# Sorted expert tiles: a ring of eight weight and row buffers instead of six, and a queue that issues a pair's weights ahead of later rows

## The reference, cut to what matters

```python
def moe_ffn(x2d, w_router, w_gate_up, w_down):      # x2d: all 2048 tokens,
    logits = x2d @ w_router                         # 192 channels
    probs = jax.nn.softmax(logits, axis=-1)
    vals, idx = jax.lax.top_k(probs, 2)
    vals = vals / jnp.sum(vals, axis=-1, keepdims=True)
    combine = jnp.sum(jax.nn.one_hot(idx, 16) * vals[..., None], axis=1)
    out = jnp.zeros_like(x2d)
    for e in range(16):
        gu = x2d @ w_gate_up[e]                     # 192 -> 2 x 384
        gate, up = jnp.split(gu, 2, axis=-1)
        h = jax.nn.silu(gate) * up
        out = out + combine[:, e:e + 1] * (h @ w_down[e])   # 384 -> 192
    return out
```

## Time and profile before

| | |
|---|---|
| runs | 1249.12, 1249.82, 1258.29 us; median 1249.82 us |
| profiled execution | 1249.4 us |
| its span | 1247.3 us |
| PE busy | 1023.5 us (82%) |
| DVE, ACT, POOL busy | 739.1, 492.8, 322.3 us |
| sorted experts, gate and up matmuls with 128 rows of weights (L2098) | 72.4 us busy, 19.8 us idle before them |

### The profile page before, as it was taken

How to read it: one execution, slowest core, us unless ns; L and a number is a source line. 1 busy time by engine, 2 the same in 40 slices (tenths; PEclk the granted TensorE clock), 3 DMA queues, 4 the chain that set the end, 5 groups by cost and what they waited for, 6 DMA issues and landing times.

```text
span 1247.3 us, 26074 instructions
## 1 busy us (share of the span) xinstructions
PE 1023.5 (82%) x9535; PEld 799.4 (64%) x9574; DVE 739.1 (59%) x2287; ACT 492.8 (40%) x1225; POOL 322.3 (26%) x516
## 2 busy tenths in 40 slices
PE   4899999999998799675888878787876668988891
PEld 3677776776776455464666657575664447888891
DVE  6586586686674244254577777777766675332334
ACT  1452452553543222032465455555554553212110
POOL 0000000000000640167444463636101213222331
PEclk8999999999998899987999999999998989999996
DMA  9152241341341999200000000000000027788875
GB/s 351 28 144 72 72 143 54 89 143 34 109 143 56 295 405 415 60 1 1 1 2 1 19 1 19 1 19 2 18 2 18 18 89 272 269 275 288 289 260 168
DMA packets 69045, 144.80 MB, mean 116 GB/s; under 512 B 4896, under 2 KB 55360, under 8 KB 66656
## 3 DMA queue, kind: packets, MB, share of 16 engines
q1 hardware_dynamic: 64352, 132.88, 31.6%
q0 software_dynamic: 4608, 10.79, 2.6%
HBM read 97.35 MB, written 46.30 MB: 115 GB/s over the span
## 4 chain that ended last, share of the span: by engine, by line
PE 39%; DVE 27%; issue 19%; ACT 6%; POOL 5%; DMA 4%; POOLq 0%; DVEq 0%; ACTq 0%; SPq 0%
DVE neg_max L714 5%; PE bank L1830 4%; PE bank L569 3%; PE bank L614 3%; PE bank L636 3%; PE bank L1967 3%; PE bank L1858 2%; PE bank L808 2%; PE bank L678 2%; DVE R L687 2%; DMA R<-in_ffn_gu 2%; PE bank L815 2%; POOL sorted_x L1069 2%; PE bank L1917 2%; ACT R L743 1%
## 5 line engine op out<-in xcount | busy, mean ns | idle before, releaser
L743 ACT ACTIVATE R<-bank,neg_max 128x128 f32<-128x128 f32 (+2 forms) x576 | 188.7, 403 | 143.8 <-DVE neg_max L714 143.7
L1057 POOL TENSOR_SCALAR R<-cf,ids_rel 128x128 bf16<-128x128 f32 x256 | 170.1, 681 | 0.3
L614 PE MATMUL bank<-cf,R 128*128 128x128 f32 x864 | 136.6, 282 | 28.9 <-ACT R L752 15.2
L714 DVE TENSOR_REDUCE neg_max<-bank 128x2 f32<-128x352 f32 (+2 forms) x216 | 129.9, 608 | 31.1 <-PE bank L597 25.5
L614 PEld LDWEIGHTS bank<-cf,R 128*128 128x128 f32 x864 | 96.6, 144 | 47.4 <-ACT R L743 33.1
L1009 POOL TENSOR_TENSOR rstd<-mean_var,cf 128x2 f32<-128x2 f32 x24 | 4.7, 194 | 461.1 <-DVE mean_var L871 461.1
L766 ACT ACTIVATE R<-bank 128x1024 bf16<-128x1024 bf16 x72 | 70.5, 1020 | 78.9 <-PE bank L569 78.5
L1830 PE MATMUL bank<-R 64*116 64x256 f32 (+1 forms) x512 | 97.8, 399 | 0.0
L569 PE MATMUL bank<-cb,R 128*128 128x128 bf16 x1008 | 70.6, 234 | 28.9 <-DVE R L554 28.8
L569 PEld LDWEIGHTS bank<-cb,R 128*128 128x128 bf16 x1008 | 65.3, 106 | 36.6 <-DVE R L554 27.3
L2098 PE MATMUL bank<-xsT,R 128*128 128x128 f32 x576 | 72.4, 279 | 19.8 <-DMA R<-in_ffn_w 19.3
(11 more groups left out here) (258 smaller groups left out, 1940.9 us busy)
## 6 DMA issues: line engine op xcount, KB each, us to landing
R<-in_ffn_w SPq DMA_DIRECT2D x48, 864.0 KB, 6.7
sorted_x<-cmp SPq DMA_DIRECT2D x8, 4128.0 KB, 15.9
R<-in_ffn_gu SPq DMA_DIRECT2D x16, 1392.0 KB, 21.0
R<-in_ffn_dn SPq DMA_DIRECT2D x16, 768.0 KB, 17.8
xs_words<-sorted_x SPq DMA_DIRECT2D x48, 129.0 KB, 4.0
R<-token_y SPq DMA_DIRECT2D x8, 384.0 KB, 6.0
rows<-R SPq DMA_DIRECT2D x8, 224.0 KB, 2.3
out_x<-x_all SPq DMA_DIRECT2D x16, 96.0 KB, 2.4
```

Source lines behind the costliest of these rows:

```text
L614: ins = nc.tensor.transpose(PT[u % 2][:, at + g * P:at + (g + 1) * P], probs[:, u % 3, g * kw + c0:g * kw + c0 + P], ident)
L714: nc.vector.tensor_reduce(neg_max[:, u % 4, 0:g], score_bank(a, u)[:, 0:g * kw].rearrange("p (g k) -> p g k", g=g), AX, ALU.max, negate=Tr ...
L743: ins = nc.scalar.activation(probs[:, u % 3, g * kw:(g + 1) * kw], score_bank(a, u)[:, g * kw:(g + 1) * kw], ACT.Exp, bias=neg_max[:, u % ...
L1057: ins = nc.gpsimd.tensor_scalar(comb_s[:, t, j, :], cst("iota_tok"), ids_rel[:, j:j + 1], None, ALU.is_equal)
```

## The change

`WRING` becomes 8: both rings get two more slots. The weights ring grows inside the large buffer `R` by 2 x 1728 words a partition, `xs_words` by 2 x 258 words. `TURN` becomes 8, so that a turn is a whole number of times round the ring: six turns instead of four.

SP's program is written anew. At the beginning it issues the weights of tiles 0 to 7 and the rows of tiles 0 to 7 without a wait for a buffer, with the weights of tile 3 ahead of rows 2; then rows 8 to 11, weights 8 to 11, and the wait for the table as before. In the loop it issues, for each pair, first the weights of t + 8 and t + 9 (each waits for `f_y` of the tile eight before) and then the rows of t + 12 and t + 13.

To stay within the memory, four work tiles of the tables have 36 entries instead of 48, and the semaphores of the weights ring are those of layer 0's ring, counted on from there (`weights_landed`). Apart from these semaphores and from the number of turns, the other engines' instructions stay as they are, in their order.

```diff
-WRING = 6
-TURN = 12
+WRING = 8
+TURN = 8
...
-        cmp2 = sb("cmp2", [P, NSORT, E1])
+        cmp2 = sb("cmp2", [P, NSORT - EARLY, E1])
...
+        def weights_landed(j, k):
+
+            pairs = len(range(j // 2, NPAIR, RING))
+            return 16 * pairs + 16 * k + 16
...
                 sp.dma_start(w1_ring[j], d["ffn1_w"][bass.ds(expert, 1)].rearrange("a p w -> (a p) w"))\
-                    .then_inc(s(f"w1_loaded{j}"), 16)
+                    .then_inc(s(f"ring{j}"), 16)
...
             for t in (0, 1):
                 load_rows(t, t)
-            for t in (1, 2):
+            for t in (1, 2, 3):
                 load_weights(t, t)
-            for t in (2, 3):
+            for t in range(2, WRING):
                 load_rows(t, t)
-            load_weights(3, 3)
-            for t in (4, 5):
-                load_rows(t, t)
-            for t in (4, 5):
+            for t in range(4, WRING):
                 load_weights(t, t)
...
-            for t in range(WRING):
+
+            def weights_ahead(t, j):
+                load_weights(t + WRING, j, lambda: sp.wait_ge(s("f_y"), t + 1))
+            for t in range(EARLY - WRING):
                 rows_ahead(t, t)
-            for t in range(WRING):
-                load_weights(t + WRING, t, lambda: sp.wait_ge(s("f_y"), t + 1))
+            for t in range(EARLY - WRING):
+                weights_ahead(t, t)
...
-            for t in range(EARLY - WRING, WRING + 4):
-                rows_ahead(t, t % WRING)
+            for t in range(EARLY - WRING, WRING):
+                rows_ahead(t, t)
...
                 for j in range(j0, TURN, 2):
+                    t = n * TURN + j
                     for r in range(2):
-                        if more or j + r + 4 + WRING < TURN:
-                            rows_ahead(n * TURN + j + r + 4, (j + r + 4) % WRING)
-                    for r in range(2):
-                        t = n * TURN + j + r
-                        if more or j + r + WRING < TURN:
-                            load_weights(t + WRING, (j + r) % WRING, lambda: sp.wait_ge(s("f_y"), t + 1))
-            f_body(0, True, WRING)
-            turns(sp, NSORT // TURN, f_body, first=1)
+                        if more:
+                            weights_ahead(t + r, j + r)
+                    for r in (4, 5):
+                        if more and (more != "last" or j + r < TURN):
+                            rows_ahead(t + r, (j + r) % WRING)
```

More of the change, by code:

```diff
@@ L357, in build @@
         cmp = sb("cmp", [P, E1, 16])
-        cmp2 = sb("cmp2", [P, NSORT, E1])
-        cmp3 = sb("cmp3", [P, NSORT, E1])
+        cmp2 = sb("cmp2", [P, NSORT - EARLY, E1])
+        cmp3 = sb("cmp3", [P, NSORT - EARLY, E1])
         slot_g = sb("slot_g", [P, 2, E1])
@@ L363, in build @@
         slots_i = sb("slots_i", [P, 2, 2], I32)
-        tile_e = sb("tile_e", [P, NSORT])
+        tile_e = sb("tile_e", [P, NSORT - EARLY])
         tile_ei = sb("tile_ei", [P, NSORT], I32)
-        tile_b = sb("tile_b", [P, NSORT])
+        tile_b = sb("tile_b", [P, NSORT - EARLY])
         tile_bi = sb("tile_bi", [P, NSORT], I32)
@@ L442, in build @@
             s(f"b_rows{j}")
-        for j in range(RING):
-            s(f"ring_gu{j}")
-            s(f"ring_dn{j}")
+        for j in range(2 * RING):
+            s(f"ring{j}")
         for r in range(2):
@@ L448, in build @@
                 s(f"{n}{r}")
-        for j in range(WRING):
-            s(f"w1_loaded{j}")
         for j in range(WRING):
@@ L907, in load_gate_up @@
             def load_gate_up(j):
-                sp.dma_start(ring_gu[j % RING], d["ffn0_gu"][j]).then_inc(s(f"ring_gu{j % RING}"), 16)
+                sp.dma_start(ring_gu[j % RING], d["ffn0_gu"][j]).then_inc(s(f"ring{2 * (j % RING)}"), 16)
             def load_down(j):
-                sp.dma_start(ring_dn[j % RING], d["ffn0_dn"][j]).then_inc(s(f"ring_dn{j % RING}"), 16)
+                sp.dma_start(ring_dn[j % RING], d["ffn0_dn"][j]).then_inc(s(f"ring{2 * (j % RING) + 1}"), 16)
             for j in range(2):
@@ L971, in rows_ahead @@
                 load_rows(t + WRING, j, lambda: (sp.wait_ge(s("f_xT"), t + 1), sp.wait_ge(s("f_place"), t + 1)))
-            for t in range(WRING):
+            def weights_ahead(t, j):
+                load_weights(t + WRING, j, lambda: sp.wait_ge(s("f_y"), t + 1))
+            for t in range(EARLY - WRING):
                 rows_ahead(t, t)
-            for t in range(WRING):
-                load_weights(t + WRING, t, lambda: sp.wait_ge(s("f_y"), t + 1))
+            for t in range(EARLY - WRING):
+                weights_ahead(t, t)
             sp.wait_ge(s("e_tiles"), 2)
             sp.wait_ge(s("scattered"), 64 * B)
-            for t in range(EARLY - WRING, WRING + 4):
-                rows_ahead(t, t % WRING)
+            for t in range(EARLY - WRING, WRING):
+                rows_ahead(t, t)
             def f_body(n, more, j0=0):
                 for j in range(j0, TURN, 2):
+                    t = n * TURN + j
                     for r in range(2):
-                        if more or j + r + 4 + WRING < TURN:
-                            rows_ahead(n * TURN + j + r + 4, (j + r + 4) % WRING)
-                    for r in range(2):
-                        t = n * TURN + j + r
-                        if more or j + r + WRING < TURN:
-                            load_weights(t + WRING, (j + r) % WRING, lambda: sp.wait_ge(s("f_y"), t + 1))
-            f_body(0, True, WRING)
-            turns(sp, NSORT // TURN, f_body, first=1)
+                        if more:
[3 more added lines that the diff above has]
+                            rows_ahead(t + r, (j + r) % WRING)
+            f_body(0, True, EARLY - WRING)
+            with sp.Fori(1, NSORT // TURN - 2) as n:
+                f_body(n, True)
+            f_body(NSORT // TURN - 2, "last")
             for r in range(2):
@@ L1910, in b_gate_up @@
                     w = ring_gu[j % RING]
-                    pe.wait_ge(s(f"ring_gu{j % RING}"), 16 * (j // RING) + 16)
+                    pe.wait_ge(s(f"ring{2 * (j % RING)}"), 16 * (j // RING) + 16)
                     if r == 0:
@@ L1943, in b_body @@
                     w = ring_dn[j % RING]
-                    pe.wait_ge(s(f"ring_dn{j % RING}"), 16 * (j // RING) + 16)
+                    pe.wait_ge(s(f"ring{2 * (j % RING) + 1}"), 16 * (j // RING) + 16)
                     for c in range(DC0):
@@ L2093, in f_gate_up @@
                 for r in range(2):
-                    pe.wait_ge(s(f"w1_loaded{(j + r) % WRING}"), 16 * (n * (TURN // WRING) + (j + r) // WRING) + 16)
+                    pe.wait_ge(s(f"ring{(j + r) % WRING}"), weights_landed((j + r) % WRING, n * (TURN // WRING) + (j + r) // WRING))
                     w = w1_ring[(j + r) % WRING]
```

## The result

| kernel | runs | median us | lowest to highest | ratio to before [95%] |
|---|---|---|---|---|
| before, in the same comparison | 20 | 1250.72 | 1247.41 to 1259.95 | |
| the change | 20 | 1245.31 | 1229.51 to 1255.29 | 0.9923 [0.9901, 0.9944] |
| the change, second comparison | 6 | 1246.29 | 1241.81 to 1251.52 | 0.9923 [0.9895, 0.9951] |

The ratios leave out executions more than 1.5% above the fastest of the same kernel, which are five of the change's first 20 and no other here; the medians and the lowest and highest times leave out none. By the ratio the change makes the kernel 0.8% faster. By the medians it is 0.4% in the first comparison (5.4 us) and 0.7% in the second, from which nothing is left out (8.4 us, against 1254.69 for the kernel before).

A forecast was written before the change was run, and what follows sets the result against it. It took weight loads asked for too late as what holds PE in the sorted experts' stage. Gains of 23.7 us less 1.9 (table) and 1.9 (scatter) gave 19.9 off 1249.4, so 1230 us, range 1224 to 1243.

The forecast's parts named there:

- Loop, lead: Steady loop: weights asked for earlier, right at `f_y`, arrive before PE wants them; gain 19.0 us, lower bound nothing.
- the slow matmuls: Loop before the change: 24 matmuls of L2105 once took 2.93 us instead of 1.61; 1.3 us not counted as gain.
- Beginning: Start of the stage: weights of tiles 6 and 7 are issued earlier and land before PE wants them; gain 4.7 us.
- Loop, traffic: Steady loop: a pair's 2.23 MB takes 5.9 us at 376 GB/s, below the 6.76 us body.
- the first rival: Steady loop: the transfers set the pace at 7.4 us a body, losing 12.3 us of the gain; 1242 us, chance 0.14.
- Second and fourth rivals: Table's delay not caught up until tile 20, 1236 us, chance 0.10; lead does nothing as loads land later, 1247, 0.07.
- Rows after weights: Loop: rows issued some 2.3 us later in the body still land before PE transposes them; cost nothing.
- rows 2 and 3: Beginning: these rows, now behind the weights of tile 3, land by 1034.9, before their transposes; cost nothing, at most 3.3 us.
- The table: SP's lead is cut once by waiting for the table; tile 13's weights come late, costing 1.9 us, between nothing and 3.8.
- Scatter of y: Scatters and copy of y hide behind PE's body, except while SP catches up behind the table; 1.9 us, between nothing and 4.
- In that gap the scatter lands early: Loop: a late copy delays `f_y` and the next weights, leaving a gap for the scatter; its shortest landing is 2.3 us.
- the third rival: Loop: scatters become the bound, DVE's copy of y waits, every turn takes 8.69 us; 1261 us, chance 0.07.

The follow-up runs named there:

- two y: The change with room for a second pair of y, used by turns, against the kernel before: ratio 0.9801, median 1225.41 us.
- the weights held: The change, but the weights of t + 8 wait until POOL has issued the second scatter of pair t - 2: ratio to the kernel before 0.9841, 1232.21 us.
- three kernels with two y and eight buffers: The change with a second pair's room for y: alone, with the table's rest entered earlier, or with rows issued first; ratios to before 0.9801, 0.9786, 0.9795.
- six, weights first: The kernel before with its six buffers, but SP issues a pair's weights ahead of the rows: ratio 0.9921, 1242.42 us.
- rows first: The change with eight buffers, but SP issues a pair's rows ahead of its weights, as before: ratio to the kernel before 0.9895, 1238.06 us.
- the two held kernels: The change with weights waiting for the second scatter's issue, without and with the table's rest entered earlier: ratios to the kernel before 0.9841 and 0.9828.

## Why the prediction was wrong

- **Loop, lead (19.0 us): right.** With two y the loop takes 148.72 - 129.1 = 19.6 us less, of which 1.3 are the slow matmuls. In the change the waits for weights go as well, but the loop takes 148.58 us, only 0.1 less.
- **Beginning (4.7 us): right.** 18.27 us became 13.52. Weights 6 and 7 are among the four that SP issues from 1037.31 on.
- **Loop, traffic, and the first rival: right to reject it.** 0.90 of the DMA engines are busy at 321 GB/s, and bodies are at 6.76 us.
- **Second and fourth rivals: right to reject them.** The change waits for weights twice, at tiles 12 and 13, and no more; 3.7 us are left of 19.3.
- **Rows after weights, rows 2 and 3: right, nothing.** No matmul of L2092 waits for rows.
- **The table (1.9 us): too small.** It cost 4.2. I had SP issue its rows again 1072.7 - 1063.4 = 9.3 us ahead of PE's tile 12. In the trace they go out at 1067.96 and tile 12 would come at 1068.64 + 6.76 = 1075.4, only 7.4 us later. With two y the wait is 0.4 us: the surplus belongs to the next point.
- **"Scatter of y" (1.9 us): this step failed.** The bodies behind the table lost 15.9 us and not 1.9. The prediction let the copy come "1.4 us after the next down projection: more room than now", since the weights would land early. It took from the earlier trace rows that a scatter lands with the weights beside it, and then let PE's body set the turn. But the copy, the scatter's issue and its landing follow one another: the second scatter is issued 2.37 us after the copy, and where weights went out 0.3 us ahead of it it was seen landed 4.6 to 7.0 us after that, so the next copy can't come sooner than 7.0 to 9.4 us after the last. All of that is more than the 6.76 of a body.
- **"In that gap the scatter lands early", the argument against the third rival: half true.** In the turns with late copies it holds for a pair's first scatter (2.4 to 3.0 us). The second, issued 1.38 us later, falls behind the weights, and the copy waits for both. So a late copy is not made up for. The experiment with the weights held puts that gap back in every other turn, and that is enough.
- **The third rival was the right mechanism, with too high a price.** It had turns of 8.69 us and 1261. Bodies from tile 14 on take 7.75, since turns with a wait (9.38) stand beside others without, and 4.7 us of the beginning stay won.

The sizes add up: of the difference between the stage's predicted 181.2 - 19.9 = 161.3 us and its 176.5, y has 15.9 - 1.9 = 14.0, the table 4.2 - 1.9 = 2.3, and the 1.3 us of slow matmuls that I had left in is to be taken off: 15.0 of 15.2.

The prediction weighed two rules of the Trainium skill, page "DMA: Bandwidth & Descriptors", section "Queues, rings and completion order". By the one, that a DMA engine takes turns between its queues packet by packet, the second scatter had little to fear from the 1.77 MB in SP's queue; here its 6.8 us from issue to landing, beside 2.35 for the first, speak against it as the whole story. By the other, that an increment lands after every earlier write of its engine, a landing is tied to the weights under way; 6.8 us behind the weights and 2.35 ahead of them agree with it. I gave that one 7 in 100. Whether write order or the queues' turns make the 6.8 us no run here tells apart.

Open: why the change's executions spread over 1229.51 to 1255.29 us, while each of the three kernels with two y and eight buffers stays within 5.6 to 7.3 us. Two profiles of the change agree in kind, but both are of executions above the median, at 1247.21 and 1251.52 us, and none is of one near 1230: what the fast executions do is not known, and the 15.9 us are those of a slower one. The other kernel with weights first, one pair of y and nothing held (six, weights first) spreads widely too, 17.1 us in 8 executions, while rows first and the two held kernels stay within 4.1 to 5.8 us in 5 or 6. That fits a spread that comes with the waits for y, but it is an argument, not shown.

## What to carry to other kernels

When loads are issued earlier, list every other transfer that the same event sets off and see which is issued first: a small store issued 0.3 us behind the first of 1.77 MB of loads took 4.4 us longer to land than its twin issued 1.04 us ahead of them. If its source has one buffer, its turn (copy, issue, landing) sets the pace once it is longer than the engine's body. Either give it a second buffer (here 384 words a partition for 1.2% more) or let the loads wait until it is issued (0.8%).

## What the runs showed of the hardware

Two things I had not expected. Two 128x192 scatters issued 1.38 us apart land after very different times: in the nine turns of the change whose weights went out 2.02 to 2.05 us after the copy, the first, about 1.04 us ahead of the weights, was seen landed after 2.4 to 3.0 us, the second, about 0.34 us behind, after 4.6 to 7.0. It is not that whichever is issued first wins. In this turn of the change the second scatter was 0.41 us ahead of the weights and still was seen landed only after 5.5 us:

```profile
1163.41 0.99 POOL L1103 DMA_INDIRECT token_y<-y_f,place_i  x1 [0.16 <-POOL scratch L1102]
1163.82 1.49 SPq L949 DMA_DIRECT2D R<-in_ffn_w  x2
...
1168.93 0.16 DVE L1769 TENSOR_TENSOR place_i<-places,cf 128x1 int32<-128x1 f32 x1 [3.89 <-DMA token_y<-y_f,place_i]
```

How far ahead a scatter has to be was not measured.

And some of the new waits cost more than their brackets, since PE's granted clock fell behind them. The stretches of the change around its waits behind the table, and before and behind those of 2.35 and 2.47 us for y:

```profile
1078.00:1084.00 6.00, 3.90 (x44) 3.47 (x44) 0.76 (x3) 0.49 (x1) 2.36 (x4) 1.00 0.99 371
1139.00:1147.00 8.00, 5.89 (x59) 5.41 (x57) 0.97 (x6) 1.53 (x4) 1.41 (x3) 1.00 0.78 273
1147.00:1155.00 8.00, 7.76 (x58) 7.64 (x60) 2.45 (x10) 0.29 (x1) 2.54 (x5) 0.79 0.68 222
1186.00:1192.00 6.00, 4.99 (x54) 4.51 (x52) 0.16 (x1) 1.53 (x4) 0.70 (x1) 1.00 0.89 307
1193.00:1199.00 6.00, 5.55 (x31) 5.55 (x32) 2.19 (x10) 0.00 (x0) 2.36 (x4) 0.72 0.42 139
```

The means of 0.79 and 0.72 lie between the two levels of 2.4 and 1.2 GHz: part of the stretch ran at the lower one. Twelve matmuls of L2118 took 2.97 and 3.62 us there and not 2.22, and the next 24 of L2102 in one case 3.79 and not 2.84. It is no matter of the wait's length alone: the clock stayed at 1.00 after the two waits behind the table (first row, 1.63 and 2.10 us), and before the change after one of 2.57.
